# A head pipeline made one head deeper: third score buffer, counts and score fetch one turn earlier, the shift first in GpSimd's turn

## What is computed

```python
dots = einsum('bhij,hk->bkij', q @ k.T * scale, pre_proj)
dots = where(causal, neg, dots)
vk = top_k(dots, 64)[0][..., -1:]          # 64th largest of each row
attn = softmax(where(dots < vk, neg, dots))
attn = einsum('bhij,hk->bkij', attn, post_proj)
out = einsum('bhij,bhjd->bhid', attn, v)
```

## Time and profile before

| what | before |
|---|---|
| three timed runs, median | 1031.14 us (1031.12 to 1031.69) |
| profiled execution | 1030.79 us |
| its span, first to last instruction | 1029.1 us |
| busy: TensorE, VectorE, ScalarE, GpSimd | 903.0, 836.7, 727.5, 487.2 us |
| granted TensorE clock, mean | 0.957 |
| first `rinv` (L1124) to the last, 64 heads | 190.26 to 854.79 us |

### The profile page before, as it was taken

The page is one execution under the profiler, slowest core; times in us unless marked ns, Lnnn a source line. Parts: engine busy times, 40 slices in busy tenths (PEclk is TensorE's granted clock), DMA queues, the critical chain, the costliest instruction groups (busy, mean ns, idle before and its releaser), DMA issues.

```text
span 1029.1 us, 16288 instructions
## 1 busy us (share of the span) xinstructions
PE 903.0 (88%) x4151; PEld 579.7 (56%) x4151; DVE 836.7 (81%) x2931; ACT 727.5 (71%) x1868; POOL 487.2 (47%) x1113
## 2 busy tenths in 40 slices
PE   8866778899999999999999999788899779899998
PEld 4623435566666666666666666566666556433432
DVE  4587994999999899999999999989999884446344
ACT  6332325899999999999999999878999684311211
POOL 2000003677777677767777777556777561000000
PEclk9768989899999999999999999999999899999999
DMA  5865130000000000000000000000000000000000
GB/s 156 151 126 92 60 33 1 2 2 2 2 2 2 2 2 2 2 2 2 1 2 1 2 2 2 2 1 2 1 2 2 1 2 1 1 0 11 11 0 21
DMA packets 15007, 18.16 MB, mean 18 GB/s; under 512 B 2656, under 2 KB 12192, under 8 KB 14240
## 3 DMA queue, kind: packets, MB, share of 16 engines
q1 hardware_dynamic: 14880, 16.85, 7.9%
HBM read 11.08 MB, written 5.77 MB: 16 GB/s over the span
## 4 chain that ended last, share of the span: by engine, by line
PE 28%; DVE 23%; ACT 23%; issue 13%; POOL 6%; POOLq 6%; DVEq 1%; DMA 0%; ACTq 0%
DVE Ex L1121 7%; ACT Ex L761 5%; ACT unread L750 5%; ACT unread L742 4%; DVE Sx L1031 4%; ACT unread L734 3%; ACT turned L769 3%; POOL spread L1362 3%; PE bFGI L456 3%; PE bBC L565 2%; POOLq L1325 2%; PE bA L565 2%; PE bFGI L574 2%; PE bFGI L566 2%; PE bBC L566 2%
## 5 line engine op out<-in xcount | busy, mean ns | idle before, releaser
L1343 POOL TENSOR_TENSOR mixed<-Sx,nthr 128x528 f32<-128x528 f32 (+3 forms) x256 | 186.2, 759 | 11.6 <-issue 11.6
L456 PEld LDWEIGHTS bFGI<-spread,Ex 128*128 128x128 f32 x1280 | 156.3, 199 | 54.2 <-POOL spread L1362 52.5
L456 PE MATMUL bFGI<-spread,Ex 128*128 128x128 f32 x1280 | 161.4, 284 | 18.2 <-POOL spread L1362 18.2
L470 PE MATMUL bH<-turned 128*128 128x512 f32 (+3 forms) x512 | 153.2, 442 | 25.1 <-ACT turned L769 24.7
L742 ACT ACTIVATE unread<-Sx,nthr 128x144 bf16<-128x144 f32 (+3 forms) x256 | 143.9, 563 | 20.1 <-POOL nthr L1324 19.2
L1121 DVE SCALAR_TENSOR_TENSOR Ex<-mixed,yk,Ex 128x144 f32<-128x144 f32 (+3 forms) x256 | 147.2, 627 | 1.7 <-DVE yk L1145 1.0
L750 ACT ACTIVATE unread<-mixed,least 128x528 bf16<-128x528 f32 (+3 forms) x256 | 143.4, 565 | 0.0
L470 PEld LDWEIGHTS bH<-turned 128*128 128x128 f32 x512 | 92.1, 189 | 86.5 <-issue 66.2
L761 ACT ACTIVATE Ex<-Sx,nmax 128x144 f32<-128x144 f32 (+3 forms) x256 | 125.5, 563 | 0.0
L1070 DVE MAX8 top<-mixed 128x8 f32<-128x528 f32 (+3 forms) x256 | 110.7, 492 | 0.0
L1362 POOL TENSOR_TENSOR spread<-ident,rinv 128x512 f32<-128x512 f32 x64 | 66.6, 1040 | 70.5 <-DVE rinv L1124 70.5
(11 more groups left out here) (348 smaller groups left out, 1735.0 us busy)
## 6 DMA issues: line engine op xcount, KB each, us to landing
heads_store<-per_head SPq DMA_DIRECT2D x2, 1152.0 KB, 5.0
mixed<-heads_store SPq DMA_DIRECT2D x16, 144.0 KB, 11.0
mixed_store<-mixed SPq DMA_DIRECT2D x2, 1152.0 KB, 4.2
per_head<-mixed_store SPq DMA_DIRECT2D x16, 144.0 KB, 6.2
xr<-in_xT SPq DMA_DIRECT2D x4, 256.0 KB, 3.5
w_s<-in_w12T SPq DMA_DIRECT2D x1, 1024.0 KB, 14.2
outT<-xc SPq DMA_DIRECT2D x4, 256.0 KB, 2.0
wq_s<-in_WqT SPq DMA_DIRECT2D x1, 512.0 KB, 3.9
```

The source lines that it names most:

```text
L456: last = mm(bFGI[:, k * P:k * P + P], Ex[g % 2][:, t, a:a + P], spread[:, t, :], start=True, stop=True)
L470: last = mm(bH[:, jt * P:T], u[:, jt, :], PT[:, at:at + n], start=h + jt == 0, stop=False)
L1343: Gp.tensor_tensor(y[ph][t], Sx[ph][:, t, 0:NT[t]], nthr[ph][1][:, t:t + 1].broadcast_to((P, NT[t])), ALU.add).then_inc(sem("y_ready"), 1)
```

## The change

The buffers `Sx` and `nmax` become three; room for them comes from laying `hsilu`, `decay` and one `unread` buffer over buffers that are idle then. Each engine's loop begins a turn earlier and is put in a new order. In turn g:

- VectorE: flip(g), nearest(g), fetch(g+3) tiles 2 and 3, read_hits(g) to add_tops(g), fetch tile 0, last_kept(g), fetch tile 1, measure_first(g+3), redo, measure_others(g+3), keep(g), tally(g+3).
- GpSimd: shift(g+1), pick_last(g), second_threshold(g+2), weigh_memory(g-1), stage(g+4), first_threshold(g+3), third_threshold(g+2), spread_scale(g).
- ScalarE: key_copy(g+4), count(g+1), value_copy(g), turned_copy(g-1), tally(g+2), weigh(g+1), first_tally(g+3).
- TensorE: turn_weights(g-1), projected(g), found(g), the two wide score tiles of head g+4, values(g-1), the two narrow ones, keys(g+5).

No instruction's operation or size changes except that `count` writes its unread output as float32; one score fetch more runs ahead of the first head, one less behind. The diff, cut to the buffers, the waits and the four loops:

```diff
-        decay = sb("decay", [P, T])
+        spread = sb("spread", [P, TT, P])
+        decay = spread[:, :, :].rearrange("p t n -> p (t n)")
...
-        hsilu = sb("hsilu", [P, 2, FI])
...
-        Sx = [sb(f"Sx{i}", [P, TT, W]) for i in range(2)]
+        Sx = [sb(f"Sx{i}", [P, TT, W]) for i in range(3)]
+        hsilu = Sx[2][:, :, :].rearrange("p t n -> p (t n)")[:, 0:2 * FI].rearrange("p (i f) -> p i f", i=2)
...
-        spread = sb("spread", [P, TT, P])
...
-        unread = [sb(f"unread{i}", [P, STOT], BF16) for i in range(3)]
+        unread = [sb(f"unread{i}", [P, STOT], BF16) for i in range(2)]
+        unread_last = work[:, :, :].rearrange("p t n -> p (t n)")[:, 0:STOT]
...
-        nmax = [sb(f"nmax{i}", [P, TT]) for i in range(2)]
+        nmax = [sb(f"nmax{i}", [P, TT]) for i in range(3)]
...
-            def scores(g):
+            def scores_wide(g):
                 b, h = divmod(g, H)
                 k = Y[g % 2]
...
                 pe.wait_ge(sem("y_copied"), g + 1)
                 if g:
                     pe.wait_ge(sem("fetched"), TT * (g - 1) + 2)
-                for t in range(TT):
-                    x_t = xn[:, b, t * P:t * P + P]
-                    if t == 2 and g:
-                        pe.wait_ge(sem("fetched"), TT * g)
-                    if t < 3:
-                        last = mm(scores_in[t], x_t, k[:, 0:NT[t]], start=True, stop=True)
-                    else:
-                        mm(scores_in[3][:, 0:MEM], x_t, k[:, 0:MEM], start=True, stop=True).then_inc(sem("s_done"), 1)
-                        last = mm(scores_in[3][:, MEM:W], x_t, k[:, MEM:W], start=True, stop=True)
-                    if t in (1, 3):
-                        last.then_inc(sem("s_done"), 1)
+                mm(scores_in[2], xn[:, b, 2 * P:3 * P], k[:, 0:NT[2]], start=True, stop=True)
+                mm(scores_in[3][:, 0:MEM], xn[:, b, 3 * P:4 * P], k[:, 0:MEM], start=True, stop=True).then_inc(sem("s_done"), 1)
+                mm(scores_in[3][:, MEM:W], xn[:, b, 3 * P:4 * P], k[:, MEM:W], start=True, stop=True).then_inc(sem("s_done"), 1)
+
+            def scores_narrow(g):
+
+                b, h = divmod(g, H)
+                k = Y[g % 2]
+                if g:
+                    pe.wait_ge(sem("fetched"), TT * g)
+                for t in range(2):
+                    last = mm(scores_in[t], xn[:, b, t * P:t * P + P], k[:, 0:NT[t]], start=True, stop=True)
+                last.then_inc(sem("s_done"), 1)
...
-            for g in range(-2, HEADS + 1):
+            for g in range(-3, HEADS + 1):
                 if g == 1:
                     pe.wait_ge(sem("ln_out"), 3 * B)
                 if 0 <= g - 1:
...
                     pe.wait_ge(sem("yk_ready"), HEADS)
                     mean4(2)
                 if 0 <= g < HEADS:
+                    projected(g)
                     found(g)
-                    projected(g)
+                if 0 <= g + 4 < HEADS:
+                    scores_wide(g + 4)
                 if 0 <= g - 1:
                     values(g - 1)
-                if g and g % H == 0:
+                if g > 0 and g % H == 0:
                     turn_memory(g // H - 1)
-                if 0 <= g + 3 < HEADS:
-                    scores(g + 3)
-                if g + 4 < HEADS:
-                    keys(g + 4)
+                if 0 <= g + 4 < HEADS:
+                    scores_narrow(g + 4)
+                if g + 5 < HEADS:
+                    keys(g + 5)
...
-            for g in range(-2, HEADS + 1):
-                if g == -1:
-                    tally(0)
-                if g + 3 < HEADS:
-                    key_copy(g + 3)
-                if 0 < g + 1 < HEADS:
-                    tally(g + 1)
-                if g == -1:
+            for g in range(-3, HEADS + 1):
+                if g + 4 < HEADS:
+                    key_copy(g + 4)
+                if 0 <= g + 1 < HEADS:
+                    count(g + 1)
+                if 0 <= g < HEADS:
+                    value_copy(g)
+                if 0 <= g - 1:
+                    turned_copy(g - 1)
+                if 0 <= g + 2 < HEADS:
+                    tally(g + 2)
+                if g == -2:
                     squares(2, (B - 1,))
                     act.wait_ge(sem("ln_inv"), 3 * B)
                     nc.scalar.activation(rstd[:, TT:], rstd[:, TT:], ACT.Sqrt).then_inc(sem("ln_root"), 1)
-                if 0 <= g - 1:
-                    turned_copy(g - 1)
                 if g == HEADS:
                     squares(3, (2,))
                 if 0 <= g + 1 < HEADS:
                     weigh(g + 1)
-                if 0 <= g < HEADS:
-                    value_copy(g)
                 if g > 0 and g % H == 0:
                     memory_copies(g // H - 1)
-                if 0 <= g + 1 < HEADS:
-                    count(g + 1)
-                if 0 <= g + 2 < HEADS:
-                    first_tally(g + 2)
-                if g == -2:
+                if 0 <= g + 3 < HEADS:
+                    first_tally(g + 3)
...
             def free_for_fetch(g):
-                if g >= 2:
-                    dve.wait_ge(sem("exp_done"), TT * (g - 1))
-                    dve.wait_ge(sem("counted"), g - 1)
+                if g >= 3:
+                    dve.wait_ge(sem("exp_done"), TT * (g - 2))
+                    dve.wait_ge(sem("counted"), g - 2)
             def fetch(g, tiles):
                 for t in tiles:
                     if t != 1:
-                        dve.wait_ge(sem("s_done"), 3 * g + (1, 0, 2, 3)[t])
-                    V.tensor_tensor_reduce(out=Sx[g % 2][:, t, 0:NT[t]], in0=scores_in[t], in1=causal[:, W - NT[t]:W], scale=DOWN, scalar=LOW,
+                        dve.wait_ge(sem("s_done"), 3 * g + (3, 0, 1, 2)[t])
...
             def flip(g):
-                if g + 2 < HEADS:
-                    dve.wait_ge(sem("s_done"), 3 * (g + 2) + 1)
+                if g + 3 < HEADS:
+                    dve.wait_ge(sem("s_done"), 3 * (g + 3) + 3)
                 dve.wait_ge(sem("counted"), g + 1)
...
-            for g in range(-2, HEADS):
-                there, coming = 0 <= g, g + 2 < HEADS
+            for g in range(-3, HEADS):
+                there, coming = 0 <= g, g + 3 < HEADS
                 if g == 0:
+                    dve.wait_ge(sem("s_done"), 3 * (g + 3) + 3)
                     V.tensor_copy(steer_p, steer_s[:, 5, :]).then_inc(sem("steer_moved"), 1)
                     dve.wait_ge(sem("steer_moved"), 1)
                 if there:
...
                             normed(2, b, ln3_bank[b])
                     if g > H and g % H == 1:
                         take_sum(g // H - 1)
+                if coming:
+                    free_for_fetch(g + 3)
+                    fetch(g + 3, (2, 3))
+                if there:
                     read_hits(g)
                     pick_tops(g)
                     add_tops(g)
                 if coming:
-                    free_for_fetch(g + 2)
-                    fetch(g + 2, (0,))
+                    fetch(g + 3, (0,))
                 if there:
                     last_kept(g)
                 if coming:
-                    fetch(g + 2, (1, 2))
-                    measure_first(g + 2)
-                    fetch(g + 2, (3,))
+                    fetch(g + 3, (1,))
+                    measure_first(g + 3)
                 if there:
                     dve.wait_ge(sem("yk_ready"), g + 1)
                     redo_missed(g)
                 if coming:
-                    measure_others(g + 2)
-                if g == -1:
+                    measure_others(g + 3)
+                if g == -2:
                     centre3(B - 1)
                     for b in range(1, B):
                         deviation(2, b, ln3_bank[b])
...
                     dve.wait_ge(sem("yk_ready"), g + 1)
                     keep(g)
                 if coming:
-                    tally(g + 2)
-                if g == -2:
+                    tally(g + 3)
...
-            for g in range(-3, HEADS):
+            for g in range(-4, HEADS):
                 if 0 <= g + 1 < HEADS:
-                    second_threshold(g + 1)
+                    shift(g + 1)
+                if g >= 0:
+                    pick_last(g)
+                if 0 <= g + 2 < HEADS:
+                    second_threshold(g + 2)
                 if g >= 1:
                     weigh_memory(g - 1)
-                if g >= 0:
-                    pick_last(g)
-                if g + 3 < HEADS:
-                    stage_memory_keys(g + 3)
-                if 0 <= g + 1 < HEADS:
-                    third_threshold(g + 1)
-                    shift(g + 1)
-                if 0 <= g + 2 < HEADS:
-                    first_threshold(g + 2)
-                if g == -1:
+                if g + 4 < HEADS:
+                    stage_memory_keys(g + 4)
+                if 0 <= g + 3 < HEADS:
+                    first_threshold(g + 3)
+                if g == -2:
```

(21 more changed lines are left out.)

31 lines of the change are left out of this document (17 added, 14 removed).

## The result

| | before | after |
|---|---|---|
| timed runs, median | 1031.4 us (1031.1 to 1037.2) | 1138.1 us (1135.3 to 1141.0) |
| ratio, 95% interval | | 1.102 (1.097 to 1.107) |
| profiled execution, its span | 1030.8, 1029.1 us | 1135.3, 1133.5 us |
| first `rinv` to the last | 190.3 to 854.8 us | 194.3 to 957.6 us |

A forecast was written before the change was run, and what follows sets the result against it. VectorE, ScalarE and TensorE were all taken as nearly full (94.6, 93.4, 93.0 of 100 us). On the profiled 1030.8 us, sixty turns at +1.64 (+98), memory turns -4 and +0.5 gave 1125 us; range 1085 to 1160.

The forecast's parts named there:

- The collision: VectorE's flips and GpSimd's shift exclude each other for whole instructions; nearest starts 2.09 us later in short turns, 1.84 in long.
- Alternation: Shift tiles and flips take turns; last flip ends at R+4.68 (short) or 4.85 (long), R being the turn's rinv start.
- rival (a): VectorE keeps the port pair through its four flips once it has it: +1.1 us a turn, 1093 us; chance 0.12.
- (b): GpSimd keeps the port pair through shift; flips begin at R+4.15, turn 12.4 us, 1160 us in all; chance 0.08.
- (c): Large VectorE and GpSimd instructions don't exclude each other, only the fixed start-up does: -0.23 us a turn, 1012 us; chance 0.14.
- (d): The greater depth does nothing, since VectorE is full either way: 1031 +- 2 us; chance 0.03.
- The short turn: Turn whose opening VectorE tally has two tiles (long: three): 10.42 us + 2.09 - 0.45 - 0.51 + 0.27 = 11.82.
- The branch: VectorE's gap after yk at the redo branch, less covered by fetches than before: +0.27 us a turn, between 0 and 0.4.
- covered by 0.4; gone if the fetches come later: TensorE's narrow scores, which flip newly awaits, are done at R+12.2, before the next away wants them at 12.6.
- The memory turns: Three turns with memory work, now 12.22 us, 2.0 too much; 0.7 to 1 left of that: 3 x -1.2 = -4 us.
- The ends: A third fetch and its tally before the first flip cost about 3 us; one turn less with a fetch returns 2.5.
- The signs: Trace marks if right: turns 11.5 to 12 us, flips over 1 in long turns, four-tile keep 2.07, ScalarE waiting for GpSimd.

The follow-up runs named there:

- e3: Changed kernel, order untouched, with the four flips written as tensor_tensor and their flip word read from PSUM: 1050.9 us, ratio 1.018.
- e13: e12 with GpSimd's shift moved ahead of second_threshold, behind pick_last, third_threshold and the stage copy: 1046.8 us, ratio 1.015.
- e2: Changed kernel with TensorE's narrow scores of head g+4 ahead of values(g-1): 1128.5 us, ratio 1.094.
- e4: Changed kernel with pick_last ahead of shift on GpSimd and measure_others ahead of the redo branch on VectorE: 1104.6 us, ratio 1.072.
- e7: e3 with measure_others ahead of the redo branch on VectorE: 1053.9 us, ratio 1.023.
- e5: Changed kernel with GpSimd's shift fifth, behind pick_last, second_threshold, weigh_memory and stage: 1131.4 us, ratio 1.098.
- e9: e5 with measure_others ahead of the redo branch and TensorE's narrow scores ahead of values: 1140.6 us, ratio 1.107.
- e12: e9 with GpSimd's third_threshold(g+1) behind the pick, a turn later than the change has it: 1124.1 us, ratio 1.092.

## Why the prediction was right, point by point

- **The collision.** Right, and shown by e3, which keeps the order and takes the claim away (-87 us). e13 keeps the claim and takes the order away (-91, or -82 from e2, whose order on TensorE it shares); it moves more than `shift` alone, so it agrees rather than proves. Alternation was the right choice of order. Under rival (a) only the flip that meets `shift` first would grow, and the second one grew as well (719 ns); under (b) the flips would stand behind `shift`'s end, and in the long turn the first is issued 2 us before it, the four being done 0.4 us after it. Rivals (c) and (d) fell with the result. In the long turn shown (R = 551.69) `flips` ends at R+2.35 and the last flip at R+4.79; the sum had 2.35 and 4.85.
- **The short turn, in part luck.** The delay of `nearest` was put at +2.09 (short) and +1.84 (long). On the mean of 27 plain turns each it is +2.32 and +1.75, but 1.25 of the 2.32 is `away` waiting for TensorE, and only 1.07 is collision. The forecast had that wait covered. The two overlap, so one stands in for the other: in e2, where the wait is gone, `nearest` is late by 1.95 and 1.72, close to the forecast of both, and the turns take 11.60 and 11.78 us. In the changed kernel a plain short turn takes 11.95 us (forecast 11.82), a long one 11.81 (11.89), with single turns from 11.3 to 12.8; a plain turn grew by 1.64 on the mean of 54, as forecast.
- **Keep clear of the shift.** Right: 573.68 to 575.76 is 2.08 us, as in the earlier trace rows.
- **The hits.** Right: no wait stands ahead of L1081 from 300 to 600 us.
- **The branch.** +0.27 was taken, with 0.4 as the upper end. The turns shown have 0.48, but from 300 to 600 us the gap sums to 9.2 us in 25 turns, 0.37 on the mean: near 0.5 in 16 turns and near 0.16 in 9. What decides between the two stays open. It can't be won back by the move of e4 and e7: one more instruction of 0.55 us in front of the branch doesn't cover it, though the two wide fetches of the kernel before did.
- **TensorE, "covered by 0.4; gone if the fetches come later".** The cover was gone: in 14 of 25 turns, mostly short ones, `away` waited, 0.2 to 1.9 us. The wide scores start where the forecast has them, at R+7.69 for 7.5; the step took the 4.69 us of the earlier trace rows for the work behind them, and it took 6.5. TensorE ahead of the short turn's `away`, and the wide pair one turn later:

```profile
559.38 1.11 PE L440 MATMUL bBC<-Y,xn 128*128 128x400 f32 x2 [1.75 <-DVE rmax L1035]
...
560.57 2.05 PE L442 MATMUL bBC<-Y,xn 128*128 128x512 f32 x2
562.42 2.80 PE L473 MATMUL bH<-turned 128*128 128x512 f32 x8
565.05 0.87 PE L451 MATMUL bA<-Y,xn 128*128 128x144 f32 x4
...
572.46 1.11 PE L442 MATMUL bBC<-Y,xn 128*128 128x512 f32 x2
```

Busy time over two stretches; the granted clock is the third number from the end:

```profile
560.00:563.00 3.00, 3.00 (x6) 1.44 (x5) 2.53 (x13) 3.00 (x9) 1.24 (x3) 0.50 0.01 3
564.00:576.00 12.00, 10.54 (x61) 7.87 (x60) 9.83 (x37) 8.63 (x23) 7.54 (x17) 1.00 0.00 1
```

TensorE waits 0.93 us for the pick (at 557.36) and 1.75 us for the fetch, and from 560 to 563 us half the clock is granted, the lower level (1.2 GHz): the 512-column pair takes 2.05 us. A turn later, at the upper level and after a single wait of 1.46 us, it takes 1.11. From the wide scores to the end of the narrow ones 6.5 us pass. The idle time of TensorE was forecast, the clock and the wait of `away` that it leads to weren't. That wait replaced part of the collision instead of adding to it, so that it was worth only the 10 us of e2.
- **The memory turns.** The one term that was wrong in its working. The text gives such a turn 2.0 us of excess over a plain one and leaves it 0.7 to 1 of them, so by its own figures 12.7 us instead of 12.22, +0.5 each. The sum left these three out of the sixty and then took 1.2 off each, -4 where its own reasoning gave +1.5. Measured +1.7 in all, 1.4 of it in the third.
- **The ends.** A third fetch ahead of the first flip: 3 us expected, 4.0 measured. The 2.5 us given back at the end show as last turns that grow by 2.5 in all instead of 4.9; behind the last `rinv` another 1.6 us come on top, not foreseen.
- **The redo turns.** +2.1 each instead of 1.64.
- **The signs.** Turns of 11.5 to 12, `keep` at 2.08, a longer `shift` and TensorE idle before the wide scores all came. Two didn't: `flips` takes 0.74 us on the mean of the plain long turns, not over 1 (the sum's own figures give 2.35 - 1.51 = 0.84), and ScalarE hardly waits for GpSimd's `shift` (1.5 us from 300 to 600 us) but 42.5 us for TensorE's keys. Of L1068 only the widest tile has a mean in the 0.8 to 1.2 us named.

Together: memory 5.7, ends 2.6, redo 1.3 and small change make up the 10 us by which 1125 missed the profiled 1135.3; the timed median lies another 2.9 above that one.

## What to carry to other kernels

Moving an instruction to an earlier place on one engine changes what it stands beside on the others. Before a reorder, list for each pair of VectorE and GpSimd instructions that will newly overlap whether they exclude each other; the smallest instruction can pay most, because it waits for the other's whole length. Where they must overlap, give one of them a form that doesn't contend, even a slower one. And when one stage is moved within a hand-written order, follow every ring it is part of once around, across all engines: e5, e9 and e12 took the collision of the flips with `shift` away and lost about the same time to a ring.
